# Attention on one Trainium2 core: weighted sums in two halves per key tile, largest scores turned on VectorE and placed by DMA, sums inverted as a 128x16 table, output kept by feature

## What is computed

```python
Q, K, V = (lora_linear(x, W, b, A, Bm).reshape(4, 2048, 16, 16) for each)
scores = einsum('bqhd,bkhd->bhqk', Q, K) / sqrt(16) + slopes[h] * (k - q)
attn = softmax(scores, axis=-1)
out = einsum('bhqk,bkhd->bqhd', attn, V).reshape(4, 2048, 256)
x = x + rezero * lora_linear(out, Wo, bo, Ao, Bo)
```

## Time and profile before

| | |
|---|---|
| median of 3 runs | 5530.03 us (5528.84 to 5532.87) |
| the profiled execution, its own time | 5538.16 us |
| its span, first to last instruction | 5536.6 us |
| PE busy | 5050.3 us (91% of the span) |
| DVE busy | 4260.3 us (77%) |
| ACT busy | 3129.3 us (57%) |
| POOL busy | 1234.6 us (22%) |
| mean granted TensorE clock | 0.936 of full speed |

### The profile page before, as it was taken

The page is one execution under the profiler, slowest core; times in us unless marked ns, Lnnn a source line. Parts: engine busy times, 40 slices in busy tenths (PEclk is TensorE's granted clock), DMA queues, the critical chain, the costliest instruction groups (busy, mean ns, idle before and its releaser), DMA issues. The chain is left out here.

```text
span 5536.6 us, 90370 instructions
## 1 busy us (share of the span) xinstructions
PE 5050.3 (91%) x27025; PEld 2717.2 (49%) x27025; DVE 4260.3 (77%) x6749; ACT 3129.3 (57%) x5877; POOL 1234.6 (22%) x959
## 2 busy tenths in 40 slices
PE   5849999999999999999999969996899999956998
PEld 3723333333333333333333357775565565645666
DVE  4757888888888888888888868887888888973000
ACT  1316777787777777777777723332454454432111
POOL 1310000000000000000000033333566666643222
PEclk8959999999999999999999989998899999856999
DMA  4950222022220222202222021112000000044443
GB/s 137 295 115 16 36 58 35 27 35 36 58 35 27 35 36 58 35 27 35 36 58 35 4 74 46 46 46 66 14 19 26 18 19 26 18 146 143 148 145 102
DMA packets 226889, 327.80 MB, mean 59 GB/s; under 512 B 58515, under 2 KB 176526, under 8 KB 216696
## 3 DMA queue, kind: packets, MB, share of 16 engines
q1 hardware_dynamic: 214300, 264.56, 20.2%
q0 software_dynamic: 12224, 58.43, 2.9%
HBM read 195.90 MB, written 134.59 MB: 60 GB/s over the span
## 5 line engine op out<-in xcount | busy, mean ns | idle before, releaser
L672 DVE TENSOR_REDUCE at_mxp<-at_ps_m 128x2 f32<-128x1024 f32 x2098 | 2463.5, 1220 | 345.0 <-PE at_ps_m L731 339.4
L622 ACT ACTIVATE at_prob<-at_ps_s 128x512 f32<-128x512 f32 x4100 | 2115.3, 602 | 482.9 <-PE at_ps_s L721 481.1
L721 PE MATMUL at_ps_s<-at_qs,at_ks 51*128 51x512 f32 x4100 | 1434.8, 474 | 12.7 <-ACT at_prob L622 2.0
L721 PEld LDWEIGHTS at_ps_s<-at_qs,at_ks 51*128 51x128 f32 x4100 | 571.7, 184 | 1259.2 <-ACT at_prob L622 1123.7
L739 PE MATMUL at_ps_o<-at_prob,at_vs 128*32 128x512 f32 x8192 | 1096.0, 607 | 0.0
L731 PE MATMUL at_ps_m<-at_ks,at_qs 49*128 49x512 f32 x4196 | 954.1, 427 | 82.8 <-DMA at_vs<-t_v 52.1
L556 POOL TENSOR_TENSOR at_onorm<-at_otok,at_rec 128x256 f32<-128x256 f32 x65 | 40.3, 620 | 2245.3 <-DVE at_rec L687 2245.3
L731 PEld LDWEIGHTS at_ps_m<-at_ks,at_qs 49*128 49x128 f32 x4196 | 423.6, 188 | 171.6 <-DVE at_mxp L672 83.0
L2326 ACT ACTIVATE ex_hid<-ex_ps_h,ex_b 128x512 f32<-128x512 f32 x128 | 88.0, 687 | 388.9 <-PE ex_ps_h L2342 380.7
L739 PEld LDWEIGHTS at_ps_o<-at_prob,at_vs 128*32 128x32 f32 x8192 | 161.4, 108 | 256.3 <-ACT at_prob L622 189.5
L1517 DVE SCALAR_TENSOR_TENSOR sc_cv<-sc_xc,sc_conv_w,sc_cv 128x512 f32<-128x512 f32 x255 | 265.9, 1074 | 21.2 <-issue 7.1
(11 more groups left out here) (310 smaller groups left out, 6245.6 us busy)
## 6 DMA issues: line engine op xcount, KB each, us to landing
t_parts<-pr_parts SPq DMA_DIRECT2D x64, 512.0 KB
ex_w<-in_fw SPq DMA_DIRECT2D x32, 1024.0 KB
at_qs<-t_parts SPq DMA_DIRECT2D x102, 256.0 KB
at_ks<-t_parts SPq DMA_DIRECT2D x102, 256.0 KB
t_buf<-at_blank POOLq DMA_DIRECT2D x8, 3076.0 KB, 9.2
at_vs<-t_v SPq DMA_DIRECT2D x17, 1024.0 KB
ex_rest<-t_buf SPq DMA_DIRECT2D x16, 1026.0 KB
t_v<-pr_vaug SPq DMA_DIRECT2D x64, 256.0 KB, 4.7
```

Of the source, the lines that this page charges most:

```text
L622: nc.scalar.activation(prob[0 if n is None else (t + 1) % 2][:, j, :], bank[:, :], ACT.Exp).then_inc(s_read, 1)
L672: nc.vector.tensor_reduce(out[:, s4, k + i, 2 * pair:2 * pair + 2], ps_m[i][:, :, :], AX.X, ALU.max).then_inc(mx_read, 1)
L721: nc.tensor.matmul(bank[:, :], ks[s][a:a + QROWS, j // 2, t1 * P:(t1 + 1) * P], qs[s][a:a + QROWS, j // 2, c * T:(c + 1) * T], start=True, ...
```

## The change

Attend. PE's order in a step becomes: scores 0, scores 1, max 0, weighted for queries 0 to 255, scores 2, scores 3, max 1, weighted for queries 256 to 511. The transposes of the sums and of the largest scores on PE are gone, and so are ACT's copies of them; all slots of the ring are scores now.

The largest scores: DVE itself turns the 128x32 table in blocks of 32x32 one step after `negate` (`turn`, which waits for POOL's lower part), SP stores the result to DRAM, waits, and reads it from there into the rows of `qs` by four DMAs.

The sums: `osum` stays with features in partitions. SP copies the four rows of sums by four DMAs into a table of 128x16, POOL takes the power -1 of it, SP stores that to DRAM, waits, and reads it back by four DMAs that spread each head's row over 16 partitions; POOL multiplies 128x512 numbers, and SP stores four blocks. All of this stands in one queue of SP in the order below. POOL clears the expert buffer by 64 smaller DMAs. The loops of all engines unroll 16 chunks (TURNS = 4) where they unrolled 8 (DVE: 2).

The loads: a band is a third of the rows of Q and K. Of the next unit, band 0 is loaded in chunk 0, band 1 behind that chunk's `store_max`, band 2 in chunk 1, V in chunk 2, V under a semaphore of its own, for which only the first weighted sum of a unit waits. At the very start all bands come before V.

Project: V's bias is added by DVE as V is written to `vaug` (four instructions of 128x256 for each chunk of 512 tokens in place of two copies of 128x512). Mix: the output is loaded by feature straight into `oT`, the 8 transposes and ACT's two copies a chunk are gone; the loads wait for `proj_done`.

```diff
 # attend, POOL
                 def normalise(n, r, m):
-                    pool.wait_ge(rec_done, n + 1)
-                    pool.wait_ge(o_stored[r], 16 * m)
-                    nc.gpsimd.tensor_tensor(onorm[r]..., otok[:, :, :, 0:HD], rec[...].to_broadcast([P, SUB, HPG, HD]), ALU.mult)
+                    pool.wait_ge(sums_in, 16 * HPG * (n + 1))
+                    nc.gpsimd.tensor_tensor(total[:, :], total[:, :], minus[:, :], ALU.pow).then_inc(inverted, 1)
+                    pool.wait_ge(weight_in, 16 * HPG * (n + 1))
+                    pool.wait_ge(o_stored[r], 16 * HPG * m)
+                    nc.gpsimd.tensor_tensor(onorm[r][:, :], osum[:, :], weight[:, :], ALU.mult).then_inc(norm_done, 1)
...
+                        nc.gpsimd.dma_start(d["buf"][ds(n * P, P), :], blank[:, :]).then_inc(cleared, 16)
                         normalise(n, r % 2, up * (CH // 2) + r // 2)
                         cut_largest(n + 1)
 # attend, SP
+                def shift_sums(n):
+                    wait_alone(sp, o_out, n + 1, always)
+                    for j in range(HPG):
+                        sp.dma_start(total[32 * j:32 * j + 32, :], osum[32 * j + HD:32 * j + HD + 1, :]...).then_inc(sums_in, 16)
+                def spread_weights(n, r):
+                    wait_alone(sp, inverted, n + 1, always)
+                    sp.dma_start(d["inverse"][r]..., total[:, :]).then_inc(inverse_out, 16)
+                    wait_alone(sp, inverse_out, 16 * (n + 1), always)
+                    for j in range(HPG):
+                        sp.dma_start(weight[32 * j:32 * j + HD, :], d["inverse"][r, j, :].partition_broadcast(HD)).then_inc(weight_in, 16)
+                def store_max(n, r, s, c):
+                    wait_alone(sp, turned, n + 1, always)
+                    sp.dma_start(d["largest"][r]..., nturned[:, :]).then_inc(turned_out, 16)
+                    wait_alone(sp, turned_out, 16 * (n + 1), always)
+                    for j in range(HPG):
+                        sp.dma_start(qs[s][row:row + 2, j // 2, c * T:(c + 1) * T], d["largest"][r]...).then_inc(max_in, 16)
...
+                            shift_sums(n)
+                            spread_weights(n, c % 2)
+                            if c < 2:
+                                load_band((u + 1) % UNITS, 1 - s, 2 * c)
+                            elif c == 2:
+                                load_values((u + 1) % UNITS, 1 - s)
+                            store_rows(n, c % 2)
+                            store_max(n + 1, (c + 1) % 2, s if c < QC - 1 else 1 - s, (c + 1) % QC)
+                            if c == 0:
+                                load_band((u + 1) % UNITS, 1 - s, 1)
 # attend, ACT: take_sums also waits for norm_done of the chunk before; take_rows and take_tokens are gone
 # attend, DVE
-                    nc.vector.reciprocal(rec[:, :, :], otok[:, :, :, HD]).then_inc(rec_done, 1)
+                def turn(n):
+                    dve.wait_ge(turned_out, 16 * n)
+                    dve.wait_ge(neg_cut, n + 1)
+                    nc.vector.transpose(nturned[:, :], nparts[:, :, :, :]...).then_inc(turned, 1)
...
                             if t == NEXT:
-                                negate(n + 1, 1 - r)
+                                negate((r + 1) % 2)
+                            if t == NEXT + 1:
+                                turn(n + 1)
 # attend, PE
-                                scores(n, t, 0, *nxt)
-                                scores(n, t, 1, *nxt)
-                                max_scores(*best, 0)
-                                scores(n, t, 2, *nxt)
-                                max_scores(*best, 1, (1, 0))
-                                scores(n, t, 3, *nxt)
-                                if t == 0:
-                                    pe.wait_ge(o_out, n + 1)
-                                weighted(n, s, t)
+                            scores(up, r, t, 0, *nxt)
+                            scores(up, r, t, 1, *nxt)
+                            max_scores(*best, 0)
+                            if t == 0:
+                                pe.wait_ge(o_out, n + 1)
+                                if c == 0:
+                                    pe.wait_ge(v_in[s], 16 * (up * (LU // 2) + uu // 2 + 1))
+                            weighted(up, r, s, t, 0)
+                            scores(up, r, t, 2, *nxt)
+                            scores(up, r, t, 3, *nxt)
+                            max_scores(*best, 1)
+                            weighted(up, r, s, t, 1)
 # mix, PE: the loop
-                        attention_rows(i + 1, m1, h1)
                         pe.wait_ge(mT_out, i + 1)
```

More of the change, by code:

```diff
@@ L508, in attend_phase @@
         kq_in = [sem(f"kq_in{s}") for s in range(2)]
+        v_in = [sem(f"v_in{s}") for s in range(2)]
         ones_set = [sem(f"ones_set{s}") for s in range(2)]
@@ L517, in attend_phase, with bank_of, place @@
         NEXT = 2 * TILES - LEAD
-        T_SUMS, T_INV, T_ROWS = 2, 4, NEXT + 4
         assert TILES == KT
-        NLD = 4 * len(CUTS) + HPG + 1
-        turn = []
-        for t in range(KT):
-            turn += [("sums", t)] * (t == T_SUMS) + [("rows", t)] * (t == T_ROWS) + [(j, t) for j in range(HPG)]
-        JOBS = len(turn)
-        assert JOBS % RING == 0
-        FIRST = ["rows"] + list(range(HPG))
-        PLACE = {name: len(FIRST) + k for k, name in enumerate(turn)}
-        def place(n, what, t):
-            k = FIRST.index(what) if n is None else PLACE[what, t]
-            return (k if n is None else n * JOBS + k), ps_s[k % RING]
+        NLD = 4 * len(CUTS) + HPG
+        LU = 4
+        TURNS = UNITS // LU
+        CH = LU * QC
+        JOBS = HPG * KT
+        LOOP = CH * JOBS
+        def bank_of(k):
+            return (k + (LOOP % RING == 1 and k >= LOOP // 2)) % RING
+        def place(up, n, t, j):
+            k = (n * KT + t) * HPG + j
+            if up is None:
+                return j, bank_of(LOOP - HPG + j), 0
+            back = next(a for a in range(1, LOOP) if bank_of((k - a) % LOOP) == bank_of(k))
+            return HPG + up * LOOP + k, bank_of(k), back
         def tile(t):
@@ L593, in _ @@
                 sp.wait_ge(ones_set[0], 1)
-                load(0, 0)
+                for r in range(len(CUTS)):
+                    load_band(0, 0, r)
+                load_values(0, 0)
                 sp.wait_ge(ones_set[1], 1)
-                sp.wait_ge(s_read, place(None, "rows", 0)[0] + 1)
-                store_max(0, 0)
-                with loop(nc, sp, 0, UNITS // 2) as up:
-                    for s in range(2):
-                        u = up * 2 + s
-                        wait_alone(sp, o_done, u * QC, always)
-                        load((u + 1) % UNITS, 1 - s)
+                store_max(0, 0, 0, 0)
@@ L604, in _ @@
+                with loop(nc, sp, 0, TURNS) as up:
+                    for uu in range(LU):
+                        s = uu % 2
+                        u = up * LU + uu
                         for c in range(QC):
                             n = u * QC + c
[L606 to L609 removed]
@@ L624, in take_sums @@
                 def take_sums(n):
+                    act.wait_ge(norm_done, n)
                     act.wait_ge(o_done, n)
                     nc.scalar.copy(osum[:, :], ps_o[:, :]).then_inc(o_out, 1)
-                def take_rows(n, first):
-                    i, bank = place(n, "rows", T_ROWS)
-                    act.wait_ge(s_done, i + 1)
-                    if not first:
-                        act.wait_ge(max_in, (n + 1) * 16 * HPG)
-                    nc.scalar.copy(nrows[:, :], bank[0:2 * HPG, :]).then_inc(s_read, 1)
@@ L637, in take_tokens @@
-                def take_tokens(n, last):
-                    i, bank = place(n, "sums", T_SUMS)
-                    act.wait_ge(s_done, i + 1 if not last else UNITS * QC * JOBS + len(FIRST) + 1)
-                    act.wait_ge(norm_done, n)
-                    nc.scalar.copy(otok[:, :, :, :].rearrange("p s j c -> p (s j c)"), (bank if not last else ps_s[LASTB])[:, :]).then_inc(s_read, 1)
-                LASTB = len(FIRST) % RING
                 act.wait_ge(always, 1)
-                take_rows(None, True)
@@ L729, in max_scores @@
                     q0 = c * T + s4 * P
-                    for a in order:
+                    for a in range(2):
                         last = nc.tensor.matmul(ps_m[i][:, a, :], qs[s][a * 64:a * 64 + MXR, pair, q0:q0 + P],
@@ L818, in mix_phase @@
         xin = [sb(f"xin{h}", [P, SUB, D]) for h in range(2)]
-        oin = [sb(f"oin{h}", [P, SUB, G, HPG * HD]) for h in range(2)]
         st, mv = sb("st", [P, SUB, 6]), sb("mv", [P, SUB, 2])
@@ L824, in mix_phase @@
         xh2 = sb("xh2", [P, SUB, D])
-        oT = sb("oT", [P, KD, T])
+        oT = [sb(f"oT{h}", [P, KD, T]) for h in range(2)]
         hT = [sb(f"hT{h}", [P, KD, T]) for h in range(2)]
@@ L1099, in _ @@
             def _(act):
-                def attention_rows(n):
```

(6 more changed lines are left out.)

254 lines of the change are left out of this document (113 added, 141 removed).

## The result

The kernel after takes **5365.18 us** (median of four runs, 5363.83 to 5378.05) against 5531.45 for the kernel before on the same chip: a ratio of 0.970, with a 95% interval of 0.969 to 0.971. Forecast were 5307, with a range of 5190 to 5460. Profiled, the span went from 5536.6 to 5362.3 us, 174 less where 223 were expected.

A forecast was written before the change was run, and what follows sets the result against it. PE's work order was taken as the bound, making PE wait for ACT and DVE for PE. Terms -214 (63 attention chunks), -18, -5, +14, -2, +2 gave -223: 5538 profiled to 5315, median 8 lower, 5307 us; range 5190 to 5460.

The forecast's parts named there:

- The step: Attention: a half-step of 1.23 us, a step of 2.45 us against 2.60 before.
- (b): Attention, once a chunk: the first weighted sum still waits for ACT's copy of the last sums, 0.4 us on PE.
- (c): Attention, once a chunk: `negate` (0.62 us) and `turn` (0.25) on DVE, of which some 0.2 us reach PE.
- the order of the bands matters only once, in the first chunk: Attention loads: band order counts only in the very first chunk, where the first gap was to shrink by 18 us.
- Nothing gained by the halves: Attention rival: scores wait for ACT in both halves, step stays 2.60 us, about 5459 us; chance 0.12.
- DVE becomes the bound: Attention rival: pairs follow closer, step 2.27 us, chunk 37.2, about 5144 us; chance 0.10.
- Twice as many changes: Attention rival: each new change between row pairs and column strips waits 0.16 us, step 2.77, about 5630 us; chance 0.06.
- The chain of SP is late: Attention rival: SP's chain, counted at 15.7 us, ends past 20; at 26, about 5690 us; chance 0.05.
- The tail: Attention's end, from ACT's last copy to the next phase: 19.3 us against 5.7, +14 us.
- The start: Attention's start: the first product no longer waits for V, the last quarter of the load, -5 us (-3 to -8).
- The stop should go: First attention chunk: DVE's 10.75 us stop during the unit's load vanishes, first gap near 45 us, -18 us.
- The term of -2: Mix: removing transposes opens PE's wait for ACT's mask copy, leaving 0.1 us a chunk gained, -2 us (0 to -15).

The follow-up runs named there:

- c: Kernel after, with ACT's exponentials on 256 of 512 queries, the other half never computed: 5352.2 us (single run).
- d: Kernel after, with DVE's maxima over 256 of 512 keys and exponentials at scale 0: 5362.2 us (single run).
- e: Kernel after, with exponentials on 256 of 512 queries and maxima over 256 of 512 keys: 5371.4 us (single run).
- b: Kernel before, with only the weighted sum in halves and the new step order, the unit's load still issued at once: 5535.87 us, ratio 0.999.
- k: Kernel before, with the new order in halves and the unit's load cut into four 1 MB parts over two chunks: 5409.55 us, ratio 0.978.
- l: Kernel before, old step order, with only the unit's load cut into four 1 MB parts over two chunks: 5526.64 us, ratio 0.999.
- h: Kernel after, with all bands and V of the next unit issued in its first chunk: 5574.7 us (single run).
- f: Kernel after, with exponentials and maxima cut to half length and PE's two blocks joined, whole weighted sum last: 5258.3 us (single run).
- g: Kernel after, with seven more stores of the inverse table on SP, each waited for: 5947.97 us (single run).
- i: Kernel after, with eight unused identity transposes in mix where the removed ones stood: 5361.68 us, ratio 0.968.
- j: Kernel after, with PE's next group of expert products in mix moved ahead of the wait for ACT's mask copy: 5343.05 us, ratio 0.965.
- a: Kernel after, with PE's old step order and one whole weighted sum: 5479.96 us, ratio 0.990.

## Why the prediction was right in kind, and 58 us too low

Of the 58 us, 49 lie between the two profiled executions (5363.8 against 5315); the other 9 are the offset to the median, taken as -8 from the kernel before and +1.4 in the kernel after.

**The step.** Right: 1.24 for a half-step against 1.23 forecast, as 0.67 + 0.57 against 0.65 + 0.58. The two hundredths are the spacing of the max pair, 0.25 in full. Runs c, d and e confirm that neither ACT nor DVE sets it. 16 steps x 0.03 are 0.5 us a chunk and 30 us in all, the larger part of what was missed in attention. The once-a-chunk costs were 0.3 instead of 0.6 and gave 17 of it back: (b) was 0.25 (13.7/55), and (c) hardly reached PE. `turn`, not in the trace of before, was taken as 0.25 and took 0.20.

**What carries the gain.** Here the working was wrong though the sum came out. It booked all of -214 to the halves and the transposes, and said that the order of the bands matters only once, in the first chunk. In the kernel before, the same halves give nothing while the load goes out at once (b), 5409.55 us when it is spread (k), and spreading alone gives 11 us (l), no more than its first gap fell. In the kernel after, issuing all at once costs 210 us (h). What I overlooked: the load at once stops PE in the new order, in 14 of 15 later units, and in the old one in none of them (63 equal gaps; the earlier trace rows, in the first chunk, is the exception). When PE stops, the clock falls, and the stop is paid more than three times (129 us for 36.6). The chance for this was put at nothing. That the same change also spread the load is why the sum came out: luck, as far as the prediction goes.

**The rivals.** *Nothing gained by the halves* fell by the step. It was true of b, by another mechanism. *DVE becomes the bound* fell: d changed nothing. *Twice as many changes* fell: the extra 0.16 us for each is not there. A change is not free either: the prediction had its price, the uncovered weight loads, inside 0.42 and 0.11, and by the estimate from f one more to and fro costs 0.34 us a step. The Trainium skill, TensorEngine Tiling (Array Packing), Key Properties, has TensorE drained at a change of tiling mode. The trace agrees so far that at a change the next weight load starts only 0.33 us behind the last products, where inside a block it starts with them; a tail of 0.16 us on top it does not show. *The chain of SP is late* fell: 4.76 us of slack against 4, and the multiply ends 2947.19 - 2933.84 = 13.35 us behind the end of the copy, against 14.7 (15.7 from the chunk's start, the copy's end put 1 us into it). g shows what it would have been: 5948 us for a chain some 8.7 us later than the slack allows, where 5690 was forecast for 6.

**The ends.** The tail was right (14.3 against 14). The start was not: from the first load to the first product 338.19 - 309.06 = 29.1 us against 31.7, 2.6 less where 5 less were expected; V is a quarter of the bytes but not of the wait. Why is open. The first gap fell by 9.8, not 18. ACT's timeline and windows behind it:

```profile
438.10 1.57 ACT L667 ACTIVATE at_prob<-at_ps_s 128x512 f32<-128x512 f32 x3 [5.91 <-issue]
```
```profile
420.00:434.80 14.80, 13.04 (x124) 4.81 (x124) 14.08 (x15) 10.67 (x20) 0.84 (x2) 1.00 0.72 118
434.80:448.50 13.70, 9.75 (x58) 3.10 (x58) 4.67 (x4) 5.92 (x11) 0.00 (x0) 0.50 0.03 4
```

The stop of 10.75 us on DVE has become one of 5.91 on ACT, beside a band instead of a unit; half clock follows for 13.7 us. "The stop should go" was wrong. The band alone does not explain it: the same bands stop nothing in the 15 later units, and what sets the first chunk apart is open. With this code unchanged, the first gap was 53.7 us in the kernel after, 58.8 in i and 63.8 in j, so it is chance within some 10 us.

**Mix.** The term of -2, with ends of 0 and -15, had the wrong sign: +10.8. Its working was right as far as it went: a chunk without a fall takes 36.8 us where it took 36.95, the 0.1 that was worked out. But a granted clock that held at 1.00 now falls to half in some chunks, nine times for 3.4 or 6.8 us in the 590 us of the window, and that is most of the loss; the single stop in the fourth chunk is the other part, some 4 us with the fall beside it (40.7 against 37.0 in i). i shows that the falls come from the hole: with it filled, 664.7 us, and eight of the nine are gone. The hole should have been priced at more than its length.

**Route**, +9.5, was not forecast, and its cause stays open. Its code is the same; it took 188 to 190 us in before, a, b, g and k, and 195 to 199 in after, c to f, h, i, j and l. Since a has nearly all of the change and stays at 188, and l has hardly any of it and shows 195, it is no step of the change as such. The traces show its chunks in one of two rhythms: some 9.2 and 9.7 us apart in turn nearly up to the end in the kernel before, 10 to 11 us from the fifth on in the kernel after. What makes it change over was not tried.

## What to carry to other kernels

Price a hole in TensorE's work by what the clock does behind it as well. Before a denser order goes in, ask what a bulk load does to it, even where the old order shows no stop at all: two edits that each measure as nothing may be one gain of 2%, so try the pair before dropping either. When work that fills a wait is removed, put other work of the same engine there (22 us here for moving one line). Where one engine feeds four, ask of each step's order which product waits alone, and reorder until the answer is none.

## What the runs showed of the hardware that I had not expected

- Engines that wait for no other engine stood still for 1.6 to 7.0 us where a load filled the DMA engines at the start of the stop and a packet of an instruction queue was near (b, h, the first chunks of after and of a, c, d, e, f, i and j); once, in the first chunk before, for 10.75 us. A short stop needs no load: one of 1.86 us on ACT, at 445.5 in the kernel before, came with the DMA engines nearly idle. With 4 MB at once 15 chunks of b were long, with parts of 1 MB two of the 63 of k and none of those of the kernel after.
- After the stops of b the granted clock was at half for 7 to 20 us. In mix, a hole of 0.67 us beside other short ones was enough for falls of 3.4 to 6.8 us, though PE was marked busy for 94% of that stretch; before, with the hole filled, there were none.
- In the same array, a change between row pairs and column strips left a weight load uncovered: 0.33 us from the last products to the next load, against 0.24 us from one pair of products to the next.
- POOL's power on 128x16 takes 2.92 us wherever it stands, as the earlier trace rows had it; `turn`, a transpose of 128x32 on DVE, takes 0.20 us; a store of a 128x16 table to memory, waited for, takes 1.93 us.
